# First attention of a two-layer network: heads paired on TensorE, exact products in three parts, output rows closed up by transfers

## The reference, cut to what matters

```python
x = L0_attn_x                                   # 4 x 1024 tokens of 256
xn = _layernorm(x)
s = _L0_attn_ref(xn, ...)                       # 16 heads of 16, sequence 1024
g = _silu(_L0_ffn_ref(xn, ...))                 # 32 experts
x = x + s * g
...                                             # second layer: other attention, other gate network

# inside _L0_attn_ref
q, k, v = (_split(lora_linear(xn, W, b, Bm, Am)) for each of q, k, v)
scores = jnp.einsum('bhqd,bhkd->bhqk', q, k) * SCALE
attn = jax.nn.softmax(scores, axis=-1)
out = jnp.einsum('bhqk,bhkd->bhqd', attn, v)
return lora_linear(out, Wo, bo, Bo, Ao)
```

## Time and profile before

| | |
|---|---|
| median of 3 runs | 3302.27 us |
| lowest and highest run | 3302.18 and 3310.47 us |
| profiled execution | 3307.49 us |
| its span, first to last instruction | 3305.7 us |
| mean granted TensorE clock | 0.982 of full |
| busy: PE, DVE, ACT, POOL | 3098.8, 2139.0, 1854.7, 1111.6 us |
| first_attention, first transfer issued; start of its last instruction | 674.67; 1530.88 us |

### The profile page before, as it was taken

One profiled execution on the slowest core, in us unless ns is written; L12 is line 12 of the kernel. 1 busy time (PEld: TensorE's weight loads), 2 busy tenths in 40 slices (PEclk: granted clock), 3 DMA queues, 4 the chain that ended last, 5 costly groups with the idle time before them and its releaser, 6 DMA issues. The chain is left out here.

```text
span 3305.7 us, 62515 instructions
## 1 busy us (share of the span) xinstructions
PE 3098.8 (94%) x21586; PEld 2208.1 (67%) x21586; DVE 2139.0 (65%) x6393; ACT 1854.7 (56%) x4670; POOL 1111.6 (34%) x1753
## 2 busy tenths in 40 slices
PE   7999999979999999996987999999999999999998
PEld 5888888822333333333776888788877888778886
DVE  5776666658888888874755555555556555555555
ACT  4666666627767767673445555455554555445553
POOL 1111111010010010002015556575555655566554
PEclk9999999979999999997999999999999999999999
DMA  4111111042223132101324434354343443244432
GB/s 137 42 41 43 40 44 37 15 83 38 51 47 67 27 71 42 29 8 55 132 75 107 98 89 96 92 121 97 79 113 86 112 98 89 65 112 101 97 83 65
DMA packets 310379, 241.68 MB, mean 73 GB/s; under 512 B 150768, under 2 KB 256688, under 8 KB 309936
## 3 DMA queue, kind: packets, MB, share of 16 engines
q1 hardware_dynamic: 310064, 237.69, 29.2%
HBM read 100.71 MB, written 39.85 MB: 43 GB/s over the span
## 5 line engine op out<-in xcount | busy, mean ns | idle before, releaser
L1660 ACT ACTIVATE b_pp<-b_pp,b_nm 128x192 f32<-128x192 f32 (+2 forms) x1024 | 472.5, 463 | 458.5 <-DVE b_nm L1828 377.0
L903 DVE TENSOR_REDUCE a_mx<-ps 128x1 f32<-128x512 f32 x1024 | 636.5, 681 | 88.3 <-PE ps L851 88.2
L825 ACT ACTIVATE a_pt<-ps 128x512 f32<-128x512 f32 x1024 | 534.9, 601 | 245.1 <-PE ps L862 243.6
L1630 POOL TENSOR_SCALAR b_pp<-b_pp,b_rc 128x192 f32<-128x192 f32 x960 | 388.0, 430 | 441.1 <-DVE b_rc L1837 441.1
L1849 DVE COPY b_pt<-ps 128x384 f32<-128x384 f32 (+2 forms) x336 | 182.0, 555 | 388.1 <-PE ps L1749 369.7
L851 PE MATMUL ps<-a_k,a_q 96*128 96x512 bf16 x1024 | 399.3, 391 | 18.9 <-DMA a_k<-qk_parts 16.1
L862 PE MATMUL ps<-a_q,a_k 99*128 99x512 bf16 x1024 | 387.4, 382 | 8.9 <-issue 5.4
L1828 DVE CUSTOM_DVE_ANT_0 b_pp<-ps,b_mk 128x192 f32<-128x192 f32 x960 | 276.3, 353 | 130.8 <-PE ps L1728 130.8
L638 DVE SCALAR_TENSOR_TENSOR f_yac<-ps,f_cw,f_yac 128x128 f32<-128x128 f32 x992 | 276.6, 343 | 122.2 <-PE ps L447 120.7
L851 PEld LDWEIGHTS ps<-a_k,a_q 96*128 96x128 bf16 x1024 | 100.1, 98 | 292.1 <-issue 152.6
L447 PEld LDWEIGHTS ps<-w,f_sq 128*128 128x128 f32 x2048 | 264.9, 191 | 29.7 <-DVE f_yac L638 7.2
(11 more groups left out here) (254 smaller groups left out, 7104.3 us busy)
## 6 DMA issues: line engine op xcount, KB each, us to landing
b_rt<-b_qf SPq DMA_DIRECT2D x1024, 64.0 KB, 2.0
qk_parts<-f_aa SPq DMA_DIRECT2D x32, 384.0 KB, 2.6
a_q<-qk_parts SPq DMA_DIRECT2D x192, 64.0 KB, 3.0
a_k<-qk_parts SPq DMA_DIRECT2D x96, 128.0 KB, 5.2
v_rows<-f_va_ SPq DMA_DIRECT2D x16, 512.0 KB, 3.0
a_v<-v_rows SPq DMA_DIRECT2D x4, 2048.0 KB, 11.6
b_raw<-in_W1qT SPq DMA_DIRECT2D x64, 128.0 KB, 2.6
b_raw<-in_W1kT SPq DMA_DIRECT2D x64, 128.0 KB, 2.8
```

What stands on the lines that cost most here:

```text
L825: e.activation(pt[(4 * i + j) % 8][:, :], P.ap(s), ACT.Exp).then_inc(P.free_sem(s), 1)
L903: e.tensor_reduce(mx[kh % 3][:, j * 4 + t, h:h + 1], P.ap(s), AX.X, ALU.max, negate=True).then_inc(P.free_sem(s), 1)
L1630: m = e.tensor_scalar(x, x, r[:, 2 * u + h:2 * u + h + 1], 1.0, ALU.mult, ALU.mult)
L1660: e.activation(x, x, ACT.Exp, bias=nm[n % 4][:, c:c + 1], scale=-1.0, accum_out=sm[n % 4][:, c:c + 1]).then_inc(exp_done, 1)
```

## The change

In words:

- `first_half`: ACT writes the rounded high part of q or k at once (type float32r), and DVE computes the rest from PSUM in one instruction (`scalar_tensor_tensor`, bias added, high part subtracted). There are two parts, not three; POOL has no part in it.
- A score product is now 48 rows: high x high, low x high, high x low, in float32r. Heads `2p` and `2p + 1` lie at partitions 0 and 64 of `qs` and `ks`. Every `max` and `score` step is two matrix products, one for each of these heads, and each on a tile of 64 rows of TensorE.
- A `max` step fills two adjoining banks (0 and 1, or 2 and 3), and one DVE reduction takes both: 128 x 2 out of 128 x 1024. There are 512 instead of 1024. The plan puts both of a step between its two pairs of scores; they run 24 ahead.
- The maxima are split in two parts by DVE alone, and four transfers lay them at rows 48 and 49 of each head. The rows of ones in `ks` are set by POOL, on 32 partitions at a time, before any load is issued (`ones_set`).
- `rows` and `three` take turns on the same pairs of banks as the `max` steps (before: banks 6 and 7). `pv` has bank 7 alone. `pt` has 12 buffers.
- `one` and `two` are gone. After `evac`, eight transfers move the 16 value rows and the 16 sum rows of each head to `og` and `sg`, closed up to 64 rows for four heads. `norm`, a new step, twice in a batch entry: DVE takes the reciprocal of `sg` (128 x 512, twice) and POOL multiplies. `three` then reads `og` directly.

```diff
@@ first_half
-                    e.activation(qf[m % 2][:, :], P.ap(s), ACT.Identity,
-                                 bias=M["bqk"][:, n, h:h + 1]).then_inc(P.free_sem(s), 1)
+                    e.activation(aa[m % 2][:, 0, :], P.ap(s), ACT.Identity,
+                                 bias=M["bqk"][:, n, h:h + 1]).then_inc(aa_high, 1)
...
+                    e.scalar_tensor_tensor(out=aa[m % 2][:, 1, :], in0=P.ap(s), scalar=M["bqk"][:, n, h:h + 1],
+                                           in1=aa[m % 2][:, 0, :].bitcast(F32), op0=ALU.add,
+                                           op1=ALU.subtract).then_inc(P.free_sem(s), 1)
@@ first_attention_plan
-        n = min(slot + 48, 36 + slot * 10 // 8, 64 * units)
+        n = min(slot + 24, 18 + slot * 10 // 8, 32 * units)
...
-        for j in range(4):
-            p += ahead(4 * i + j + 1)
-            if i + 1 < 16 * units:
-                p.append(("score", i + 1, j))
+        if i + 1 < 16 * units:
+            p.append(("score", i + 1, 0))
+        if (c == 2 or c >= 4) and side:
+            p.append(side.pop(0))
+        p += ahead(2 * i + 2)
+        if i + 1 < 16 * units:
+            p.append(("score", i + 1, 1))
         p.append(("pv", i))
         if c == 7:
             p.append(("evac", i // 8))
             if u % 4 == 3:
+                n = 2 * (u // 4) + h
+                side += [("norm", n)] + [("three", 4 * n + t) for t in range(4)]
@@ first_attention, banks
             if s[0] == "max":
-                P.take(s, s[1] % 3)
+                P.take(s, 2 * (n_max % 2), 2 * (n_max % 2) + 1)
+                n_max += 1
             elif s[0] == "score":
-                P.take(s, 3 + (4 * s[1] + s[2]) % 3)
+                for a in range(2):
+                    P.take((*s, a), 4 + n_score % 3)
+                    n_score += 1
...
+            elif s[0] in ("rows", "three"):
                 if last is None:
+                    P.take(s, 2 * (n_max % 2), 2 * (n_max % 2) + 1)
+                    n_max += 1
@@ sync
+                    w.wait_ge(ones_set, 3)
...
+                elif k == "evac":
...
+                    for j in range(4):
+                        r = slice(64 * (g % 2) + 16 * j, 64 * (g % 2) + 16 * j + 16)
+                        e.dma_start(og[h][r, g // 2, :], ev[n % 2][32 * j:32 * j + 16, :]).then_inc(og_in[h], 16)
+                        e.dma_start(sg[h][r, g // 2, :], ev[n % 2][32 * j + 16:32 * j + 32, :]).then_inc(og_in[h], 16)
@@ pool
-                e.memset(k6[i][KS:KX, :, :], 1.0).then_inc(ones_set, 1)
+                e.memset(ks[i][32:64, :, :].bitcast(F32), 1.0)
+                e.memset(ks[i][96:128, :, :].bitcast(F32), 1.0).then_inc(ones_set, 1)
@@ tensor
+                    for a in range(2):
+                        w.wait_ge(*P.before((*s, a)))
+                    for a in range(2):
+                        r = slice(64 * a, 64 * a + KX)
+                        e.matmul(P.ap((*s, a)), ks[u % 3][r, j, c * 128:(c + 1) * 128], qs[u % 3][r, h, j, :],
+                                 start=True, stop=True).then_inc(P.full_sem((*s, a)), 1)
@@ vector
-                    e.tensor_reduce(mx[kh % 3][:, j * 4 + t, h:h + 1], P.ap(s), AX.X, ALU.max,
+                    e.tensor_reduce(mx[kh % 3][:, :, jt, h], P.pair(s), AX.X, ALU.max,
                                     negate=True).then_inc(P.free_sem(s), 1)
...
+                elif k == "norm":
+                    w.wait_ge(og_in[n % 2], 512 * (n // 2 + 1))
+                    for c in range(2):
+                        x = sg[n % 2][:, c, :]
+                        e.reciprocal(x, x).then_inc(rc_ready, 1)
```

More of the change, by code:

```diff
@@ L70, in ap, with pair @@
         return self.ps[:, self.at[step][0], :]
+    def pair(self, step):
+        i = self.at[step][0]
+        return self.ps[:, i:i + 2, :]
     def full_sem(self, step):
@@ L675, in ahead @@
             emitted += 1
-            if emitted % 32 == 0:
-                out.append(("both", emitted // 32 - 1))
-                late.append((slot + (2 if slot else 0), ("rows", emitted // 32 - 1)))
+            if emitted % 16 == 0:
+                out.append(("both", emitted // 16 - 1))
+                late.append((slot + (1 if slot else 0), ("rows", emitted // 16 - 1)))
         return out
@@ L683, in first_attention_plan @@
         p.append(late.pop(0)[1])
-    p += [("score", 0, j) for j in range(4)]
+    p += [("score", 0, j) for j in range(2)]
     side = []
@@ L697, in first_attention_plan @@
             if u % 4 == 3:
+                n = 2 * (u // 4) + h
+                side += [("norm", n)] + [("three", 4 * n + t) for t in range(4)]
                 if i + 1 == 16 * units:
-                    p += side
-                    side = [("last",)]
-                f0 = 8 * (u // 4) + 4 * h
-                for n in range(6):
-                    side += [(s, f0 + n - lag) for lag, s in ((2, "three"), (1, "two"), (0, "one")) if 0 <= n - lag < 4]
-        elif 2 <= c <= 5 and side:
-            p.append(side.pop(0))
+                    side.insert(0, ("last",))
     return p + side
 def first_attention(nc, A, M, X):
-    QP = (0, 0, 1, 1, 0, 2)
-    KP = (0, 1, 0, 1, 2, 0)
-    KS, KX = 96, 99
+    parts = ((0, 1, 0), (0, 0, 1))
+    KS, KX = 48, 50
     with ExitStack() as ctx:
```

224 lines of the change are left out of this document (93 added, 131 removed).

## The result

| | before | after |
|---|---|---|
| median of 4 runs | 3303.56 us | 3414.56 us (3409.45 to 3425.07) |
| ratio of the medians | | 1.0336, 95% interval 1.0306 to 1.0366 |
| profiled execution | 3307.49 us | 3411.24 us |
| its span, mean granted clock | 3305.7 us, 0.982 | 3409.4 us, 0.951 |
| first to last group of scores (the loop) | 788.3 us | 889.1 us |

The account below looks back on a forecast made before the run. PE was taken to bound the kernel before, the chain of scores after; loop +8, start +11 and end -1 gave +18 to +19, so 3321 us, 0.6% slower, range 3262 to 3372.

Parts of the forecast that it names:

- 255 steady steps: Loop of the changed stage: 2.57 us a step, 655 us in all, against 2.85 a step before.
- `norm`, TensorE's waits for maxima behind it: Seven `norm` inside the loop: two reciprocals of 4.2 us each stop the maxima, 8.1 us each time, +57.
- first steps, `evac`, `three`, `rows`: Interruptions in the loop: first steps +6, `evac` +6, `three` +29, `rows` +28, less 2 where both share a step.
- The chain of the scores: Steady step: second score pair waits for the first exponential's bank, `pv` follows 0.32 behind; this sets 2.57 us a step.
- 2.39 + 2 x 0.09: Steady step: the old chain's 2.39 us plus the float32r weight load of 0.09, twice, makes 2.57.
- upper bound of 2.65: Steady step: 2.65 us if the second product of a pair also starts late.
- rival E: Loop: SP late with head rows; held hidden with 2.7 us to spare, else 1 us for 14 units, +14; 5%.
- One to two steps: 2 us each, +14: Loop, behind each `norm` wait: PE's clock at 0.50 for one to two steps, +14 in all.
- rival D: Loop: low clock lasts three steps or more after each `norm`, 15 to 30 us more, 3335 to 3350; 10%.
- Reciprocals under 3.5 us: `norm` on DVE: sign that would prove the forecast wrong, which took 4.2 us for a reciprocal of 512 columns.
- I take 0, between -2 and +3: `first_half`: no change in time expected, since PE sets that stage's pace.
- Rival C: Steady step: pairs don't run side by side, 2.94 us a step, 94 us more, total 3400; 7%.

Follow-up runs that it names:

- e4: Against the changed kernel: load at the seventh step behind the head rows, and reciprocals over two columns (division left out); 3308.00 us, ratio 1.0012.
- e7: Against the changed kernel: from the fourth step on exponentials take 128x256 instead of 128x512, half of the probabilities left as they were; 3386.90 us, ratio 1.0256.
- e1: Against the changed kernel: the `pv` group stands between the two pairs of scores, the maxima behind the second pair; 3405.07 us, ratio 1.030.
- e2: Against the changed kernel: the load of unit u+2 stands at the seventh step of a half, behind the head rows, not the second; 3366.85 us, ratio 1.0184.
- e11: Against the changed kernel: the eight transfers of each evacuation issued by GpSimd's queue instead of SP's, load where it was; 3379.73 us, ratio 1.0230.
- e15: Against the changed kernel: stops for head rows filled with idle products over all 128 rows of the array; 3401.53 us, ratio 1.0290.
- e3: Against the changed kernel: the sixteen reciprocals run over 128x2 instead of 128x512, so the division is left out; 3353.43 us, ratio 1.0148.
- e8: Against the changed kernel: late load, `pv` between the pairs of scores and the norm in eight pieces, work whole; 3322.64 us, ratio 1.0054.
- e9: Against the changed kernel: late load, and one row of sums a head with one reciprocal 128x64 a `norm`, spread back through memory; 3324.05 us, ratio 1.0049.
- e14: Against the changed kernel: late load, short reciprocals and exponentials of 128x256, division and half of the probabilities left out; 3273.30 us, ratio 0.9910.
- e13: Against the changed kernel: stops for head rows filled with idle products of 48 rows, wait for the rows behind them; 3418.67 us, ratio 1.0346.

## Why the prediction was wrong, step by step

The loop was forecast at 796 and took 889.1, 93 us more. Term by term; the last column rests on the trace of after and, for the clock, on e4, so that it is an estimate:

| term | forecast | found |
|---|---|---|
| 255 steady steps | 655 | 704 (2.76 each) |
| waits for head rows | 0 | 38.5 |
| low clock, start and behind stops | 17 | about 47 |
| `norm`, TensorE's waits for maxima behind it | 57 | 34 |
| first steps, `evac`, `three`, `rows` | 67 | about 66, the rest of 889 |

**The mechanism of the step was right, its size was not.** "The chain of the scores" decides, released by the first exponential, as said, and e7 shows it by shortening that exponential. The term "2.39 + 2 x 0.09" is the one mis-sized: the 2.57 is 2.76. S0 to ACT is 0.60 and not 0.51: the pair ends 0.50 behind its start, close to the 0.48 of the earlier trace rows, but ACT starts 0.10 behind that end. ACT to S1 is 0.74 and not 0.65: S1 waits in the row above, released by ACT, and nothing else is late there. Why either is 0.09 more than forecast no run shows. The upper bound of 2.65 was still too low. 0.19 x 255 = 48 us. Of the chain's form e1 says more than I saw: it has two links a step, of 1.27 (e1) to 1.34 (after) where no `pv` lies in them. By that, an estimate, no order of the same work gets much under 2.55, as long as both products of a pair wait for both of their banks before the first is issued, as the kernel has it. The warning of the Trainium skill (TensorEngine Tiling (Array Packing), PSUM Bottleneck), named in the forecast, holds here: the step lost 0.09 us of its 2.85 although the pairs run side by side in 0.50.

**The overlap that failed was that of rival E**, "SP is late with head rows", which I held for "hidden with 2.7 to spare" and gave 14 us at worst. The sum there has a slip: 13.7 + 4 x 0.6 + 1.7 is 17.8 and not 17.4, which leaves 2.3 to spare. The queue was counted in the right order, but with every price too low. An ordinary place, unit 1, shows them: the eight transfers of the evacuation take 5.0 us (783.00 to 788.03), 0.63 each and not the 0.46 of a load's (3.7); the load takes 10.1 (to 798.11, one transfer 1.5 longer than the rest) and not 8.3; four row transfers take 2.7, not 2.4; and the scores start at 803.9, 3.1 us behind the last issue, where the landing was put at 1.7. Together that is more than the 2.3 us and the 1.3 that seven longer steps give, and the scores wait 1.75. Behind the load with the values it is 10 us from 849.1 to the scores at 859.02. So the rows are 7 to 8 us late at three places and about 2 at eight others. Late load (e2) and GpSimd's queue (e11) each take away nearly all of these waits: 48 and 35 us. I had it in the list at 5%, with a bound worked out from the median landing, when the trace of before showed no case of a transfer right behind a load.

**The clock was the third.** "One to two steps: 2 us each, +14." The price of a step at the low level was fair: 4.16 us instead of 2.76. How often it is paid was not. I counted seven norms; the low level is there behind nearly every stop of TensorE of some 2 us or more, for rows as for the norm (the stop at 1488.7 is an exception), and often for more than two steps: between 740 and 1590 the clock is below 1.00 in 15 of 17 windows of 50 us. It also comes without a stop, where no maxima are left: from 1580 to 1600 it is at 0.50 to 0.51, and no wait in the 10 us before was longer than 0.84. TensorE's busy time says 47 us (e4), the filled stops say at least 13 for part of the rows alone (e15). In the difference of after and e4 there are 48 us of waits and 47 of slow matmuls, so that a microsecond of waiting cost nearly two. That is rival D, which I priced at 15 to 30.

**The norm was put too high, which hid a part of the miss.** A reciprocal of 512 columns costs 3.32 us where I took 4.2: 6.2 ns for each further element, by the times for 2, 128 and 512, which is the lower slope of the earlier trace rows. "Reciprocals under 3.5 us" was among the signs of being wrong, and it came true. The 4.4 us that I estimated from the Trainium skill (VectorE: DVE Perf Modes, First, the fixed hardware budget) is too high by a third; a repeat count of 8 was not 8 cycles for each element here. TensorE's waits behind it are 2.05 to 6.43 us in six places, not 8.1 in seven. With the clock behind them all reciprocals are worth 61 us (e3), against 57 + 14 forecast.

**Outside the loop.** The start cost 11.1 us, as forecast (+11): GpSimd's memsets are 1.80 us each, as said, by the element, all six lie between the start of the stage at 667.29 and 678.3, and the first transfer follows at 678.33, 11.04 us behind that start. What was wrong is "I take 0, between -2 and +3" for `first_half`: it is 7.4 us shorter in after, and 5.4 to 7.4 in every run of this document, all of which have the changed `first_half`. The lead grows steadily along that stage, from 1.4 us at 51 us to 7.4 at 603. The change there took instructions from DVE and GpSimd; which of these freed TensorE no run shows. The end of the stage, from the last `pv` to GpSimd's last instruction, takes 23.8 us instead of 24.7 (forecast 23.5). DVE's reductions are 1218 ns alone and 2.36 for two; forecast 1.19 and 2.26.

**Luck.** The sign came out right, but not by its sum: steps, rows and clock were put 118 us too low in all, the norm 23 too high, and `first_half` 7 too high. Rival C, 3400, comes close to the measured time, but its mechanism is absent: a pair's products start 0.003 us apart, not 0.22.

Nothing of this was a version that beats the kernel before: e8 and e9, whole, stay 0.5% above it, and e14, at 3273, leaves out the division and half of the probabilities.

## What to carry to other kernels

When a TensorE that was busy without a break gets waits, price each wait twice: once for its length, once for the clock behind it, and look for the shape (one stop of 6 us or eight of 0.8) before the sum. Count the issuing queue like an engine, at each transfer's own price and with what stands ahead of the small urgent ones: here the cure was to issue the same bytes five steps later, or from an idle queue. Check each stage between its own barriers: here 11 us lost at the start of one stage and 7 won in the one before look like 4 if only the first scores are compared. And of a ring of banks ask how many links a step takes through it; with three banks for pairs each pair waits for the pair before, in either of the orders tried here.

## What the runs showed of the hardware that was not expected

- In a filled stop TensorE's granted clock fell from 1.00 to 0.50 between 856 and 858 us while products of 48 rows ran without a pause. With products of 128 rows in the same places (e15) the windows at 740 and 1040 us stayed at 1.00, where they were 0.86 and 0.92 in e13, with products of 48 rows, and 0.86 and 0.91 in after, with none.
- TensorE's granted clock also fell to 0.50 with no stop: from 1580 us on in after, where the engine had been busy for 7.0 of the last 10 us and had waited for at most 0.84 at a time.
- A reciprocal on VectorE takes 3.32 us for 128x512 and 0.93 us for 128x128 (0.156 us for 128x2): 6.1 to 6.2 ns for each further column.
- Issue on SP's queue: 0.63 us from one transfer of 16 rows from tile to tile to the next, 0.68 for a head row, 0.47 for one of a load. GpSimd's queue issued the same transfers of 16 rows 0.48 apart (e11). The 2 MB of values moved at 387 GB/s for 4 to 5 us; head rows issued right behind their transfer (after) reached the scores 10 us after the last issue, rows issued amid their bytes (e11) within 4.5 us.
